# Decoder on one core: queries of the attention blocks sent through a DRAM scratch instead of being spread by TensorE, and block steps moved

## The reference, cut to what matters

```python
x = LN(x + self_attention(x))      # 16 heads of 8, rope, biases       block SELF0
x = LN(x + cross_attention(x,ctx)) # 16 heads of 8                     block CROSS0
x = LN(x + top2_mixture(x))        # 8 experts, 128 -> 512 -> 128      block MIX0
x = LN(x + causal_attention(x))    # one head of 128                   block CAUSAL1
x = LN(x + cross_attention(x,ctx)) # 16 heads of 8                     block CROSS1
x = LN(x + top1_mixture(x))        # 8 experts with 128 places each    last mixture
```

## Time and profile before

| | us |
|---|---|
| median of 3 runs (lowest to highest) | 437.92 (437.26 to 438.38) |
| the profiled execution, its own time | 437.39 |
| its span, first to last instruction | 435.6 |
| PE busy | 370.9 (85%) |
| DVE busy | 282.0 (65%) |
| ACT busy | 226.1 (52%) |

### The profile page before, as it was taken

One profiled execution on the slowest core, in us unless ns is written; L12 is line 12 of the kernel. 1 busy time (PEld: TensorE's weight loads), 2 busy tenths in 40 slices (PEclk: granted clock), 3 DMA queues, 4 the chain that ended last, 5 costly groups with the idle time before them and its releaser, 6 DMA issues.

```text
span 435.6 us, 8944 instructions
## 1 busy us (share of the span) xinstructions
PE 370.9 (85%) x3188; PEld 324.7 (75%) x3188; DVE 282.0 (65%) x833; ACT 226.1 (52%) x526; POOL 53.8 (12%) x61
## 2 busy tenths in 40 slices
PE   4478899999889999999968999899999789863492
PEld 3367777777779997989967999788997577632491
DVE  6388898888965557632795455844866887825353
ACT  2126476575666564766347555684557455711231
POOL 6600002920000000000000000000002002010125
PEclk9999999999999999999989999999999989975598
DMA  4547511113440000200020000200011115700301
GB/s 129 159 115 247 140 36 44 47 37 108 130 113 34 2 2 2 73 2 2 2 72 2 2 0 2 74 2 1 2 47 41 42 32 159 239 15 0 109 13 33
DMA packets 22459, 25.14 MB, mean 58 GB/s; under 512 B 3208, under 2 KB 17169, under 8 KB 22416
## 3 DMA queue, kind: packets, MB, share of 16 engines
q1 hardware_dynamic: 21184, 23.14, 18.1%
q0 software_dynamic: 512, 0.97, 0.7%
q10 hardware_dynamic: 720, 0.46, 0.3%
HBM read 17.82 MB, written 6.83 MB: 57 GB/s over the span
## 4 chain that ended last, share of the span: by engine, by line
PE 68%; DVE 17%; issue 7%; ACT 3%; DMA 2%; SPq 1%; POOL 0%; POOLq 0%; DVEq 0%; ACTq 0%
PE bank_D L847 13%; PE bank_C L737 10%; PE bank_D L711 8%; PE bank_A L722 7%; DVE negmax L1214 5%; PE bank_A L863 4%; PE bank_A L865 3%; PE bank_A L864 3%; PE bank_D L637 2%; PE bank_D L695 2%; PE bank_D L767 1%; PE bank_A L777 1%; DVE q_sp L1209 1%; PE bank_A L1518 1%; PE bank_D L750 1%
## 5 line engine op out<-in xcount | busy, mean ns | idle before, releaser
L1214 DVE TENSOR_REDUCE negmax<-bank_D 128x2 f32<-128x512 f32 x192 | 127.5, 686 | 43.0 <-PE bank_D L711 42.9
L986 ACT ACTIVATE expo<-bank_A 128x512 f32<-128x512 f32 x192 | 110.1, 597 | 53.3 <-PE bank_A L722 51.9
L711 PE MATMUL bank_D<-k_head,q_sp 128*128 128x256 f32 x384 | 90.3, 320 | 11.2 <-DVE negmax L1214 5.1
L722 PE MATMUL bank_A<-q_sp,k_head 128*128 128x256 f32 x384 | 82.0, 298 | 4.9 <-DVE q_sp L1209 3.4
L1022 ACT ACTIVATE hidden<-bank_A,b 128x256 f32<-128x256 f32 x128 | 53.7, 471 | 52.1 <-PE bank_A L865 52.0
L711 PEld LDWEIGHTS bank_D<-k_head,q_sp 128*128 128x128 f32 x384 | 61.0, 197 | 23.5 <-issue 13.0
L847 PE MATMUL bank_D<-mix_w,hidden 128*128 128x128 f32 x512 | 67.8, 275 | 0.0
L722 PEld LDWEIGHTS bank_A<-q_sp,k_head 128*128 128x128 f32 x384 | 60.0, 192 | 7.9 <-DVE q_sp L1209 5.3
L847 PEld LDWEIGHTS bank_D<-mix_w,hidden 128*128 128x128 f32 x512 | 62.5, 191 | 1.6 <-issue 1.6
L737 PE MATMUL bank_C<-expo,v_aug 128*32 128x256 f32 x768 | 48.0, 392 | 2.0 <-ACT expo L986 1.9
L1273 DVE SCALAR_TENSOR_TENSOR y_mixture<-bank_D,g_w,y_mixture 128x128 f32<-128x128 f32 x64 | 22.3, 349 | 30.5 <-PE bank_D L847 28.8
(11 more groups left out here) (174 smaller groups left out, 511.1 us busy)
## 6 DMA issues: line engine op xcount, KB each, us to landing
mix_w<-in_mix_w SPq DMA_DIRECT2D x24, 256.0 KB, 3.9
k_head<-k_scratch SPq DMA_DIRECT2D x96, 48.0 KB
k_scratch<-qk_hi SPq DMA_DIRECT2D x24, 128.0 KB, 2.3
w_last<-in_mix_w SPq DMA_DIRECT2D x8, 256.0 KB, 5.5
k_scratch<-qk_lo SPq DMA_DIRECT2D x12, 128.0 KB, 2.4
proj_w<-in_proj SPq DMA_DIRECT2D x1, 640.0 KB, 6.5
xe_scratch<-empty_row SPq DMA_DIRECT2D x1, 520.0 KB, 4.5
expo<-xe_scratch SPq DMA_DIRECT2D x2, 260.0 KB, 3.3
```

The costliest lines, as they stand in the source:

```text
L711: last = mm(where(seq, b, ("max", k))[:, qt * SEQ:(qt + 1) * SEQ], q_sps[SET[seq, b]][:, k // 4, qt * P:(qt + 1) * P], k_heads[SET[seq, b] ...
L722: last = mm(where(seq, b, ("exp", h))[:, kt * SEQ:(kt + 1) * SEQ], k_heads[SET[seq, b]][:, t, g, kt * P:(kt + 1) * P], q_sps[SET[seq, b]][ ...
L986: activate(expo[:, exp_slot(seq, b, h), :], where(seq, b, ("exp", h))[:], ACT.Exp, scale=float(HD) ** -0.5).then_inc(free(seq, b, ("exp", ...
L1214: V.tensor_reduce(negmaxes[SET[seq, b]][:, s // 4, :, 32 * (s % 4)], where(seq, b, ("max", s))[:].rearrange("p (q n) -> p q n", q=QT), AX. ...
```

## The change

The matrix `spread`, its load, its copy by ACT, the eight matmuls and two ACT copies of each block go, and with them the two A bank turns. `by_query` on the SP queue takes their place: three stores of the query parts to a scratch in DRAM, a wait for them, four loads of one group (128 partitions, 128 KB) each to `q_sp`. The first eight rows of each head in the scratch are zeros, written once for each of the two scratches by a copy from DRAM to DRAM. PE and DVE wait for the loads in pairs (`q_ready`). The query projection moves from step -6 to -10 and the low part from -5 to -9. The last attention of CROSS0 and the first CROSS1, with the last mixture, are placed 4 ticks later; the last three CROSS1 are placed 8 ticks later.

```diff
-QUERIES_AT, QUERIES_LOW_AT, QUERIES_SPREAD_AT = -6, -5, -3
+QUERIES_AT, QUERIES_LOW_AT = -10, -9
...
-             (3, SELF0, 80), (2, CROSS0, 96), (3, CROSS0, 121), (0, CROSS1, 140), (1, CROSS1, 164),
-             (2, CROSS1, 188), (3, CROSS1, 204)]
-MIXTURE = [(0, MIX0, 83), (1, MIX0, 103), (2, MIX0, 131), (3, MIX0, 156)]
+             (3, SELF0, 80), (2, CROSS0, 96), (3, CROSS0, 125), (0, CROSS1, 144), (1, CROSS1, 172),
+             (2, CROSS1, 196), (3, CROSS1, 212)]
+MIXTURE = [(0, MIX0, 83), (1, MIX0, 103), (2, MIX0, 131), (3, MIX0, 160)]
...
-                sp.dma_start(staging, ins["spread"][:, QHI:QLO + 1, :, :]).then_inc(ld_spread_q, 16)
...
+                def by_query(seq, b):
+
+                    q_rows = q_dram[SET[seq, b]]
+                    if b == SELF0:
+                        sp.wait_ge(split_q_ready[seq], 1)
+                    else:
+                        wait_drained(sp, seq, b, "q")
+                    if (seq, b) in BEFORE:
+                        for ready in q_ready[SET[seq, b]]:
+                            sp.wait_ge(ready, 32 * (ORDER[seq, b] // SETS))
+                    for kind, part in enumerate((qk_hi, qk_hi, qk_lo)):
+                        sp.dma_start(q_rows[:, (kind + 1) * HD:(kind + 2) * HD],
+                                     part[:, 0, :].bitcast(f32)).then_inc(q_stored, 16)
+                    sp.wait_ge(q_stored, 16 * KEY_KINDS * (ORDER[seq, b] + 1))
+                    sp.wait_ge(q_cleared, 16 * SETS)
+                    if (seq, b) in BEFORE:
+                        wait_filled(sp, *BEFORE[seq, b], ("exp", HEADS - 1))
+                    for t in range(GROUPS):
+                        sp.dma_start(q_sps[SET[seq, b]][:, t, :].bitcast(f32),
+                                     q_rows[head(t, 0):head(t, 3) + 1:2]
+                                     ).then_inc(q_ready[SET[seq, b]][t // 2], 16)
...
+                for q_rows in q_dram:
+                    sp.dma_start(q_rows[:, 0:HD], ins["spread"].rearrange(
+                        "(h j) k t c -> h j (k t c)", j=HD)).then_inc(q_cleared, 16)
                 for seq, b, what in TURNS:
+                    if what == "q":
+                        by_query(seq, b)
                     if what == "k":
                         by_head(seq, b)
...
-                def spread_rows(seq, b):
-
-                    for half in range(2):
-                        wait_free(pe, seq, b, f"sq{half}")
-                        for t in (2 * half, 2 * half + 1):
-                            dst = where(seq, b, f"sq{half}")[:, (t % 2) * SEQ:(t % 2 + 1) * SEQ]
-                            mm(dst, spread[:, QHI, t, :], qk_hi[:, 0, :], start=True, stop=False)
-                            last = mm(dst, spread[:, QLO, t, :], qk_lo[:, 0, :], start=False, stop=True)
-                        last.then_inc(full(seq, b, f"sq{half}"), 1)
...
                     if k == 0:
-                        wait_drained(pe, seq, b, "sq0")
+                        pe.wait_ge(q_ready[SET[seq, b]][0], 32 * (ORDER[seq, b] // SETS + 1))
...
                     if k == 8:
-                        wait_drained(pe, seq, b, "sq1")
+                        pe.wait_ge(q_ready[SET[seq, b]][1], 32 * (ORDER[seq, b] // SETS + 1))
...
                         if s == QUERIES_AT and b > SELF0:
+                            act.wait_ge(q_stored, 16 * KEY_KINDS * ORDER[seq, b])
                             high(seq, b, "q", 0, bq[b])
-                        if s == QUERIES_SPREAD_AT:
-                            spread_queries(seq, b)
...
-                act.wait_ge(ld_spread_q, 16)
-                activate(spread[:], staging, ACT.Copy).then_inc(spread_q_ready, 1)
...
                         if s == QUERIES_LOW_AT:
+                            if (seq, b) in NEXT_TO:
+                                dve.wait_ge(q_stored, 16 * KEY_KINDS * ORDER[seq, b])
```

More of the change, by code:

```diff
@@ L55 @@
 NOWHERE = 4 * TOKENS
-QHI, QLO = range(2)
 KEY_KINDS = 3
@@ L165, in attention @@
                 turn(seq, b, "q", "D")
-            if s == QUERIES_SPREAD_AT:
-                turn(seq, b, "sq0", "A")
-                turn(seq, b, "sq1", "A")
             if s == BACK_AT:
@@ L249, in constants @@
     c[:, C_TOKEN:C_TOKEN + TILES] = P * np.arange(TILES)[None, :] + np.arange(P)[:, None]
[L250 to L257, removed]
+    zeros = np.zeros((HEADS * HD, SEQ), np.float32)
+    return c, zeros
 def decoder(nc, ins, out):
@@ L272, in decoder @@
         const = sb("const", [P, C_END])
-        spread = sb("spread", [P, 2, GROUPS, P], f32r)
         proj_w = sb("proj_w", [P, len(W_NAMES), P])
@@ L298, in decoder @@
         k_dram = [nc.dram_tensor(f"k_scratch{i}", (HEADS, KEY_KINDS, HD, SEQ), f32, kind="Internal").ap()
+                  for i in range(SETS)]
+        q_dram = [nc.dram_tensor(f"q_scratch{i}", (HEADS, 32, SEQ), f32, kind="Internal").ap()
                   for i in range(SETS)]
@@ L373, in decoder @@
             sem("ld_k0"), sem("ld_q0"), sem("ld_vo0"), sem("ld_bv0"), sem("ld_p1"))
-        ld_spread_q, ld_mix_biases = sem("ld_spread_q"), sem("ld_mix_biases")
-        spread_q_ready = sem("spread_q_ready")
+        ld_mix_biases = sem("ld_mix_biases")
+        q_cleared, q_stored = sem("q_cleared"), sem("q_stored")
+        q_ready = [[sem(f"q_ready{i}_{half}") for half in range(2)] for i in range(SETS)]
         v_zeroed, k_zeroed = sem("v_zeroed"), sem("k_zeroed")
@@ L438, in wait_drained @@
             eng.wait_ge(free(seq, block, what), TURNS[seq, block, what][2] + 1)
-        staging = expo[:, 0:2, :].rearrange("p a (t c) -> p a t c", t=GROUPS)
         def exp_slot(seq, block, h):
@@ L680, in queries @@
                     project(seq, b, "q", wq[b], xT[seq], rope=(b == SELF0))
[L682 to L688, removed]
                 def shift(seq, b, t):
@@ L940, in high @@
                              ACT.Identity, bias=bias).then_inc(high_ready[seq], 1)
[L942 to L947, removed]
                 def root(seq, b):
@@ L1206, in attention @@
                             q_sp = q_sps[SET[seq, b]]
-                            wait_drained(dve, seq, b, f"sq{t // 2}")
+                            dve.wait_ge(q_ready[SET[seq, b]][t // 2], 32 * (ORDER[seq, b] // SETS + 1))
                             wait_filled(dve, seq, b, ("shift", t))
```

## The result

The changed kernel takes 501.23 us (median of 4 runs, 500.2 to 503.73), against 437.73 us: ratio 1.145, interval 1.142 to 1.149. Slower was forecast, but by 18 us and not by 63. The span is 499.5 us.

The account below looks back on a forecast made before the run. PE was taken as the bound (85% busy), sharing it with DVE in pure attention. 437.39 + 21.7 (late sixth block) - 6.2 (spreading saved) + 3.0 (moves) = 455.9, forecast 456 us, range 446 to 464 us.

Parts of the forecast that it names:

- The moves: Later placement of the last blocks and last mixture: 2.5 us at the last block plus 0.5, together 3.0 us, bounds 0 and 6.
- Rival B: First two blocks: query stores overtake the large loads, second block 10 us late instead of 17.3; 446 to 449 us, chance 0.07.
- Rival D: PE at half pace after the 8 us stand, query loads at 3.6 us: 462 to 464 us, chance 0.10.
- The new road, link by link: Queries through DRAM in each block: 3.6 us for stores, 3.0 us for query loads, bounds 2.3 and 3.6.
- the round's first term: Fourth to sixth block: 6.2 us from first score to next keys' stores, within a round of 19.7 us.
- 6.5 in the third block: Third block: its key stores come 6.5 us after the preceding first score, 7.2 before; the block was forecast 19.4 us late.
- "Nothing" for the last two CROSS1: Last two CROSS1 blocks: ten ticks, about 11.5 us, suffice for 6.6 us of transfers even behind key loads; no loss.
- The late 17.7 us: Stretch from the sixth block's first score to the end: forecast -3.2 us, with 6.2 us gained and 3.0 lost to moves.
- The page that I weighed: Skill page pricing a transfer at 2.0 us plus bytes over 436 GB/s; early bulk loads cheaper, 450 us; not followed.
- the rows: Profile rows of the kernel before, used to price transfers: query stores land at 26.4 us in the first block; forecast 456.

Follow-up runs that it names:

- the change of shape: Changed kernel with eight query loads of 32 partitions (64 KB each) instead of four over four heads, same bytes: 479.01 us, ratio 1.097 to the kernel before.
- filling the stands: Changed kernel plus 22, 13, 10, 10, 12 and 10 extra matmuls before the first score of blocks two to six and eleven: 489.42 us, ratio 1.121.
- the moves alone: Kernel before with the new placement and query steps at -10 and -9, spreading kept on TensorE: 439.7 us against 437.58, ratio 1.004.
- four blocks of twelve: Kernel before with only blocks seven to ten through DRAM, eight loads each, zero copies moved to the fourth block: 432.28 us against 436.81, ratio 0.989.

## Why the prediction was wrong

The direction was right and the size was not: 18 us forecast, 63 measured, outside the range.

**Confirmed.** The large loads hold up the query stores: forecast 26.4 us, seen 26.31. Behind `cT_all` I had priced the same effect too high: 8.5 us from its issue to the query loads, and 6.9 seen (44.93 to 51.83). Keys and queries follow each other on one issuing engine: stores, key loads and query stores took 3.6, 3.3 and 4.1 us in the fifth block, 3.6, 3.3 and 3.6 forecast. The second block's keys came 6.1 us after the first score (5.8). The moves cost 1.8 us (0.4 to 3.3), 3.0 forecast. The queries of the seventh to tenth block are hidden. Rival B, overtaking stores, is out. Rival D, the lower clock behind a long stand, named a mechanism that did take place, at a chance of 0.10 and far too small a price.

**The step that failed first** is the price in "The new road, link by link": "A query load is of 128 KB like a store, so I price it like one". I looked at bytes and not at shape. The store goes over 128 rows, the load over four heads, and uses a quarter of the DMA engines (share 0.26). In place of 3.0 us (bounds 2.3 and 3.6) it took 5.6 to 6.2. Over the first six blocks this term alone is 17.2 of the 24.5 us by which the sixth block came later than forecast; the change of shape took 22 us off the whole time.

**The second** is the round's first term, "I take 6.2" from first score to the next keys' stores, and 6.5 in the third block. It was 9.2, 7.8, 7.5 and 8.9 us, together 8.4 us more. Part of that was no news: in the kernel before the same four are 7.2, 5.9, 7.0 and 7.5 us, and my 6.2 came from the shortest of them. That is 2.5 us. The other 5.9 are new. I had reasoned that DVE has caught up during the stand and had left the clock to rival D, for the one long stand, at 3 to 4 us. The fall came after every stand, and filling the stands brought the four back to 26.9 us together, where the kernel before has 27.6. The two terms are 25.6 us; the other links together, `cT_all` most of all, give 1.1 us back.

**The third** is "Nothing" for the last two CROSS1. The eleventh block shows why: its query projection on PE, the end of its low part on DVE, and its query stores and loads on SP.

```profile
377.65 0.59 PE L653 MATMUL bank_D<-xT_all,proj_w 128*128 128x256 f32 x2
```

```profile
380.58 0.42 DVE L1093 SCALAR_TENSOR_TENSOR qk_lo<-bank_D,qk_hi 128x256 fp32r<-128x256 f32 x1
```

```profile
384.64 1.17 SPq L582 DMA_DIRECT2D q_scratch<-qk_hi  x2
...
388.26 2.25 SPq L589 DMA_DIRECT2D q_sp<-q_scratch  x4
```

The slack was as forecast: from the projection to the moment at which PE stands, 389.05 us, it is 11.4 us, forecast 11.5. The need was not 6.6 us "even behind key loads". It was 3.4 us to the low part, 3.6 behind the keys (their stores were issued only at 376.81 us, their loads at 381.33), 3.6 for the stores and 5.6 for the loads: 16.2 us, and the wait is the difference, 4.8 us. I had left out the first link, put the second at nothing and the last at 3.0. The twelfth block waited 1.59 us.

**The late 17.7 us.** Forecast were -3.2. The profile of the moves alone has 6.9 us more in this stretch than the kernel before. Set against it block by block, the changed kernel's stretch is 10.8 us longer. The rounds that end at the eleventh and the twelfth first score take 9.4 us more, with the 6.4 us of waits in them and a granted clock of 0.82 instead of 1.00 between the two scores. Between the sixth and the eighth first score it loses 3.0 us, between the eighth and the tenth it gains 3.2, where the spreading is saved, and it loses 1.6 at the end. PE is busy 6.8 us longer with fewer matmuls, 3.7 of them already in the moves alone. How much each single fall of the clock cost there was not measured; one, from 222 to 229 us, has no query wait ahead of it, and the moves alone have one like it from 218 to 224.

**The page that I weighed.** By the Trainium skill's fixed 2.0 us and bytes over 436 GB/s the whole came to 450 us, further off than by the rows. It gives the first large loads and the query stores 23.6 us where 26.31 were measured (the rows 26.4), but behind `cT_all` it is no worse than the rows: 5.6 us, 6.9 measured, 8.5 forecast. The page gives this fit for DMAs that GpSimd issues, and these are SP's. It has no term for the number of engines either; the rule on that number, quoted above, stands on the same page, and I did not use it.

## What to carry to other kernels

Price a DMA by its access pattern before its bytes: look which dimension is outermost on both sides, and at the DMA share in a window where it runs alone. A wait on TensorE in front of dense work costs its length and then a stretch at the lower clock: the slower query load that made the tenth block's first score 2.2 us later made the eleventh's 3.8 us later. Count a transfer's slack from the moment at which its data are ready and its queue is free, not from the step that begins to make them. Moving work off a full engine pays where the other road's whole chain, with all that stands ahead of it in its queue, fits in the slack that is already there: here in four blocks of twelve, 4.5 us, while all twelve cost 63.

## What the runs showed of the hardware

- The same 256 KB from DRAM to SBUF in 1 KB rows: 3.3 us from first issue to first use over 32 rows outermost, 5.6 us over 4, 8.3 us over 2, with DMA shares of 0.49, 0.26 and 0.14.
- After waits of 2.4 to 10 us TensorE was granted 1.2 GHz for the next 3 to 5 us of full work, and 2.4 GHz when the wait was filled with matmuls.
- A 128x128 by 256 matmul on the constants stood twice in the trace and took 0.43 us, while one on the split operands of the scores took 0.12 us, both at 2.4 GHz.
